# A sequence-mixing, conditioned feed-forward kernel: the fourth half's sum on VectorE, the first remainder on GpSimd, biases ahead of q, two halves scaled in parts

## What is computed

```python
q_emb = relu(cond @ W3 + b3)                       # 128 x 256
v_sum = x.sum(axis=1, keepdims=True)
x1    = (32 * x + v_sum) * q_emb[:, None, :]
c     = relu(x1 @ W2 + b2)
w1q, w3q, w2q = ternary(w1), ternary(w3), ternary(w2)   # clip(round(w / mean|w|), -1, 1) * mean|w|
h1, h3 = c @ w1q.T, c @ w3q.T                      # 682 hidden features
out   = x + (silu(h1) * h3) @ w2q.T
```

## Time and profile before

| | us |
|---|---|
| median of 3 runs | 165.37 (165.34 to 166.15) |
| profiled execution | 165.74 |
| its span, first to last instruction | 163.9 |
| TensorE busy | 159.6 (97% of the span) |
| VectorE busy | 118.7 (72%) |
| ScalarE busy | 89.2 (54%) |
| GpSimd busy | 55.2 (34%) |
| chain of work that ended last | TensorE 97%, VectorE 1% |

### The profile page before, as it was taken

The page is one execution under the profiler, slowest core; times in us unless marked ns, Lnnn a source line. Parts: engine busy times, 40 slices in busy tenths (PEclk is TensorE's granted clock), DMA queues, the critical chain, the costliest instruction groups (busy, mean ns, idle before and its releaser), DMA issues.

```text
span 163.9 us, 2289 instructions
## 1 busy us (share of the span) xinstructions
PE 159.6 (97%) x760; PEld 131.2 (80%) x760; DVE 118.7 (72%) x189; ACT 89.2 (54%) x163; POOL 55.2 (34%) x53
## 2 busy tenths in 40 slices
PE   7899999999999999999999999999999999999992
PEld 3798778888887888788887888788887888788892
DVE  2588999988978891788548891888548870566863
ACT  4068889435844375345844466355844566255540
POOL 5014033402360276205740276204841266001500
PEclk9999999999999999999999999999999999999999
DMA  4998646566566599000250007000150006000163
GB/s 123 342 345 167 97 77 100 94 98 102 84 96 97 91 217 171 2 4 0 38 90 0 0 4 125 5 0 0 30 100 4 2 0 115 13 0 0 19 113 128
DMA packets 67412, 12.67 MB, mean 77 GB/s; under 512 B 63216, under 2 KB 67144, under 8 KB 67400
## 3 DMA queue, kind: packets, MB, share of 16 engines
q1 hardware_dynamic: 67248, 12.46, 38.9%
q10 hardware_dynamic: 152, 0.07, 0.2%
HBM read 8.32 MB, written 4.19 MB: 76 GB/s over the span
## 4 chain that ended last, share of the span: by engine, by line
PE 97%; DVE 1%; issue 0%
PE bank L538 49%; PE bank L581 21%; PE bank L469 17%; PE bank L565 3%; PE bank L503 1%; PE bank L445 1%; PE bank L484 1%; PE bank L452 0%; PE bank L496 0%; DVE x L656 0%; DVE qT L744 0%; PE bank L478 0%; PE bank L443 0%; DVE xo L793 0%; PE bank L506 0%
## 5 line engine op out<-in xcount | busy, mean ns | idle before, releaser
L538 PE MATMUL bank<-c_hi,T 128*128 128x512 f32 (+1 forms) x176 | 69.2, 393 | 0.0
L538 PE MATMUL bank<-c_lo,T 128*128 128x512 f32 (+1 forms) x176 | 68.8, 391 | 0.0
L389 ACT ACTIVATE silu<-bank,checked 128x512 f32<-128x512 f32 (+1 forms) x48 | 33.1, 689 | 51.6 <-PE bank L538 51.4
L778 DVE SCALAR_TENSOR_TENSOR gf<-bank,out_scale,silu 128x512 f32<-128x512 f32 (+1 forms) x42 | 31.2, 744 | 34.5 <-PE bank L538 30.8
L538 PEld LDWEIGHTS bank<-c_hi,T 128*128 128x128 f32 (+1 forms) x176 | 32.8, 186 | 7.6 <-issue 0.2
L538 PEld LDWEIGHTS bank<-c_lo,T 128*128 128x128 f32 (+1 forms) x176 | 32.8, 186 | 7.3
L272 POOL TENSOR_TENSOR x<-y,qT 128x512 f32<-128x512 f32 x12 | 13.7, 1145 | 53.2 <-DVE y L685 53.2
L469 PE MATMUL bank<-x,W_sb 128*128 128x256 f32 x128 | 29.5, 381 | 0.5 <-DVE x L656 0.5
L581 PE MATMUL bank<-g_hi,T 128*128 128x512 f32 x70 | 28.5, 407 | 0.0
L786 DVE TENSOR_TENSOR g_lo<-gf,g_hi 128x512 fp32r<-128x512 f32 x40 | 28.4, 711 | 0.0
L396 ACT CAST g_hi<-gf 128x512 fp32r<-128x512 f32 x40 | 24.5, 612 | 5.4 <-DVE gf L778 5.1
(11 more groups left out here) (78 smaller groups left out, 111.7 us busy)
## 6 DMA issues: line engine op xcount, KB each, us to landing
xb<-in_x_dram SPq DMA_DIRECT2D x64, 64.0 KB, 2.5
out_dram<-turned SPq DMA_DIRECT2D x28, 128.0 KB, 2.7
xo<-in_x_dram SPq DMA_DIRECT2D x3, 256.0 KB, 4.0
w_sb<-in_L_ffn_w_dram SPq DMA_DIRECT2D x2, 384.0 KB, 5.1
w_sb<-in_L_ffn_w_dram SPq DMA_DIRECT2D x1, 682.0 KB, 7.5
w_sb<-in_L_ffn_w_dram SPq DMA_DIRECT2D x2, 256.0 KB
xo<-in_x_dram SPq DMA_DIRECT2D x1, 512.0 KB, 4.2
xo<-in_x_dram SPq DMA_DIRECT2D x2, 128.0 KB, 2.7
```

Source lines behind the costliest of these rows:

```text
L389: nc.scalar.activation(silu[r, m % 2, :], h1[j % 2][r], ACT.Silu, scale=checked[r, 0:1]).then_inc(silu_done, 1)
L538: last = pe.matmul(dst[j % 2][0:w, :], T13[:, k, col:col + w], part[:, g % NC, k, :], start=(i == 0), stop=(i == len(passes) - 1))
L778: nc.vector.scalar_tensor_tensor(out=gf[r, m % 3, :], in0=second, scalar=out_scale[r], in1=silu[r, m % 2, :], op0=ALU.mult, op1=ALU.mult). ...
```

## The change

- `SUMMED` has half 3 too: TensorE only transposes it, VectorE sums it over the sequence, adds the sum and scales it from `y`. This scaling moves ahead of the first limit and comparison.
- The remainder of half 0 moves from VectorE to GpSimd, where it stands behind the two `c_hi` and does not wait for the fourth scaling; the remainder of half 1 still does.
- `transpose_b` stands ahead of `project_q`.
- Halves 0 and 1 are scaled in two instructions of 256 columns, one for each block of features; TensorE starts on the first block (`first_part_done`), and does both blocks' matmuls in that order.
- The fillers read a constant that the launch sets up, and the tile `blank` and its memset go.

```diff
-    SUMMED = (1, 2)
+    SUMMED = (1, 2, 3)
...
                     if n == 0 and t == 1:
+                        transpose_b()
                         project_q()
-                        transpose_b()
...
+            def project_by_parts(n):
+
+                z = z_of(n)
+                for k in range(DC):
+                    if k:
+                        pe.wait_ge(x1_done, n + 1)
+                    else:
+                        pe.wait_ge(first_part_done, n + 1)
+                    for c in range(DC):
+
+                        last = pe.matmul(z[:, c, :], W2_sb[:, k, c * P:(c + 1) * P], x1[:, n % 2, k, :],
+                                         start=(k == 0 and c == 0), stop=(k == DC - 1), skip_group_check=True)
+                last.then_inc(z_done, 1)
...
-            pe.wait_ge(blank_ready, 1)
+            filler = nc.const_aps.tensor(1.0, [P, BANK], BF16)
             for _ in range(WARM_UP):
-                pe.matmul(bank[:, 7, :], blank[:], blank[:].unsqueeze(1).broadcast_to([P, BANK // P, P]), start=True, stop=True)
+                pe.matmul(bank[:, 7, :], filler[:, 0:P], filler, start=True, stop=True)
...
-            project_c(0)
+            project_by_parts(0)
             mix_x(2)
-            project_c(1)
+            project_by_parts(1)
...
+            def scale_by_parts(n):
+
+                if n in SUMMED:
+                    dve.wait_ge(y_done, nth_summed(n))
+                else:
+                    dve.wait_ge(mixed_done, n + 1)
+                for k, done in enumerate((first_part_done, x1_done)):
+                    whole = y[:, n % 2, k] if n in SUMMED else mixed_of(n)[:, k * HT:(k + 1) * HT]
+                    nc.vector.tensor_tensor(by_batch(x1[:, n % 2, k]), by_batch(whole),
+                                            qT[:, n, k].unsqueeze(2).broadcast_to([P, HB, S]), ALU.mult).then_inc(done, 1)
```

More of the change, by code:

```diff
@@ L99, in adaln_ternary_ffn_kernel @@
         mix = sb("mix", [P, P], F32)
-        blank = sb("blank", [P, P], BF16)
         warm = sb("warm", [P, 1], F32)
@@ L160, in adaln_ternary_ffn_kernel @@
         zeroed = sem("zeroed")
-        blank_ready, mix_ready = sem("blank_ready"), sem("mix_ready")
+        mix_ready = sem("mix_ready")
+        first_part_done = sem("first_part_done")
         condT_done, condT_copied = sem("condT_done"), sem("condT_copied")
@@ L282, in _ @@
                 nc.gpsimd.tensor_copy(half_of(c_hi, n), ct[:, n % NCT]).then_inc(first_hi_done, 1)
-            pool.wait_ge(early_lo_done, 1)
-            pool.wait_ge(x1_done, EARLY)
-            for n in range(1, EARLY):
+            for n in range(EARLY):
+                if n == 1:
+                    pool.wait_ge(x1_done, EARLY)
                 if n < HALVES:
@@ L508, in keep_busy @@
                 for _ in range(n):
-                    pe.matmul(bank[:, 7, 0:P], blank[:], blank[:], start=True, stop=True)
+                    pe.matmul(bank[:, 7, 0:P], filler[:, 0:P], filler[:, 0:P], start=True, stop=True)
             keep_busy(2)
@@ L681, in add_sum @@
                 dve.wait_ge(vsum_done, nth_summed(n))
-                if n >= EARLY:
-                    dve.wait_ge(x1_done, max(n - 1, SUMMED[-1] + 1))
+                if n > HALVES:
+                    dve.wait_ge(x1_done, n - 1)
                 nc.vector.scalar_tensor_tensor(
@@ L728, in check_scales @@
                                                ).then_inc(checked_done, 1)
-            nc.vector.memset(blank[:], 0.0).then_inc(blank_ready, 1)
             nc.vector.memset(mix[:], 0.0).then_inc(mix_ready, 1)
@@ L747, in _ @@
             parts = [slice(part[0] * D, (part[-1] + 1) * D) for part in PARTS]
-            scale_mixed(0)
+            scale_by_parts(0)
             for n in SUMMED:
@@ L751, in _ @@
                 add_sum(n)
-                scale_mixed(n)
-            early_lo(0)
+                if n < HALVES:
+                    scale_by_parts(n)
+                else:
+                    scale_mixed(n)
             limit(0)
             above_limit(0, w1_sb, w1_t, parts[0])
-            scale_mixed(3)
             limit(1)
```

4 lines of the change are left out of this document (removed).

## The result

| | before | changed |
|---|---|---|
| median of 6 runs, us | 165.91 (165.34 to 166.16) | 168.88 (168.02 to 169.62) |
| ratio, 95% interval | 1 | 1.0188 [1.0164, 1.0212] |
| profiled execution, us | 165.74 | 169.16 |
| its span, us | 163.9 | 167.4 |
| TensorE busy, us | 159.6 | 160.6 |

The changed kernel is 3.0 us slower. I had forecast 166.5 with a range up to 168.3. Its chain of work that ended last is TensorE 95% and VectorE 3%, where it was 97% and 1%.

What follows compares the result with a forecast made beforehand. TensorE, busy from the first hidden product at 16.71, bounds the end, so only earlier work matters. One hold puts that product 1.20 or 1.04 later, about 1.15 on 165.37: 166.5 us, range 165.6 to 168.3.

Steps and rivals of the forecast that it cites:

- project(0): TensorE's projection of half 0, after the first scaling at the launch; forecast to start at 6.87, 0.51 us sooner.
- two holds: Rival: GpSimd's remainders block both scale(3) and the first comparison on VectorE; 2.29 us later, 167.7 us, chance 0.35.
- the hand-over: TensorE's transpose of w1_t's first part, which waits for the first comparison; 14.19 before, forecast 15.57.
- the first hold: On VectorE, scale(3) waits until GpSimd is through with half 0's remainder; costs 1.02 us read as a lock.
- the longer chain: VectorE's added sum, addition and scaling of half 3 ahead of the first comparison; priced at 0.86 us to the hand-over.
- The new wait: Behind the hand-over: second comparison perhaps held until 16.7, ending 17.25, needed at 17.7; nothing new was forecast late.
- the second race: Whether GpSimd's second remainder (14.79) or VectorE's first comparison (14.83) starts first; GpSimd's lead 0.04 us.
- one hold: Main case: GpSimd's remainder blocks VectorE's path once, about 1.15 us; 166.5 us, chance 0.45.
- scale(3): VectorE's scaling of half 3, now from y in SBUF, ahead of the comparison; forecast about 1.7 us instead of 0.69.
- the fall of the clock: Rival: TensorE's standstill of 2 to 3 us drops its clock, up to 2 us more; 169.6 with two holds, chance 0.05.
- the launch: Work up to project(0): q's reordering makes the first scaling start 0.26 sooner, part scaling brings the gain to 0.51 us.
- Rivals 2 and 3: 2: GpSimd doesn't stop the comparison, 165.5 us, chance 0.12. 3: TensorE's earlier arrival counts in full, 164.5, faster 0.03.

Runs made afterwards that it cites:

- the longer chain alone: Kernel before with half 3 summed on VectorE and scaled ahead of the comparison, half 0's remainder on VectorE behind it: ratio 1.0076, median 166.86 us.
- the launch parts alone: Kernel before with only fillers on constants, biases ahead of q and halves 0 and 1 scaled in parts: ratios 0.9985 and 1.0008, medians 165.67 and 165.70 us.
- The repeated profile: The changed kernel run again unedited for a second profile: profiled execution 168.52 us, ratio 1.0172 over its first three executions.

## Why the prediction was wrong

**What held.** The end moves with the first hidden product: from there to the end of the span it was 147.2 and 147.7, the half microsecond being the rest of the clock's spell. VectorE's comparison became what TensorE waits for. From project(0) the way was well forecast: for two holds I had worked out 16.66 - 6.87 = 9.79 from project(0) to the hand-over; it was 9.77 and 9.78 in the two profiles. That it fits to 0.02 is in part luck, since two errors cancel: the first hold was priced at 1.02 and the second at 1.09 (16.60 - 15.51), and they measured 0.95 and 0.97; the longer chain was priced at 0.86 (14.54 - 6.87 = 7.67, where before it was 6.81) and measured 1.00 and 1.04. From hand-over to hidden product I had 2.34; it was 2.42 where the clock stayed up. The new wait that I looked for behind the hand-over didn't appear with two holds, and did when they were gone.

**The step that failed: the second race.** I took one hold as the likeliest (0.45) and two as a rival (0.35), because the second remainder would start 0.15 behind scale(3)'s end and only 0.04 ahead of the comparison. The 0.15 came from the earlier trace rows (14.48 to 14.63). In the changed kernel the remainder starts 0.08 after scale(3) is through (12.46 + 1.69 = 14.15, 14.23), and so 0.09 ahead of the comparison, as far as in the race that GpSimd wins in the earlier trace rows (12.72 and 12.82). All five profiles with both holds say the same: a lead of 0.13 for the first, of 0.08 or 0.09 for the second. Why the gap is 0.08 and not 0.15 stays open. The remainder waits for two semaphores where it waited for three, but their number is not enough: with the longer chain alone it waits for three, and starts 0.09 behind the end of what releases it (14.98 + 0.69 = 15.67, 15.76). In the four profiles with 0.14 or 0.15 the releasing scale(3) reads PSUM, in those with 0.07 to 0.09 the releasing instruction reads SBUF only; no run changes that alone. With two holds as the forecast the time would have been 167.7, still within the range; what took the time out of it are the next two.

**The second: the fall of the clock.** It had 0.05 and was left outside the range. Its price was about right (up to 2.0; in the first profile 1.06 up to the hidden product, 3.48 less 2.42, and 0.5 behind it; but the three executions at 0.980 took 3 us more than those beside them). Its chance was far too small: by the mean clock six of twelve executions have it. And it should have been tied to the holds, since it was seen only with their standstill. The range's end at 168.3 leaves out four of the six executions without a fall, and all with one.

**The third: the launch.** Project(0) was forecast at 6.87, 0.51 sooner. The profiles with all launch parts give 6.41, 7.30, 6.41, 6.68, 6.95, 6.88 and 7.79, with the launch parts alone 7.36 and 7.50; the kernel before gives 7.38 and its variants 7.40, 6.83 and 7.26. I read one execution as if the pace's rise and the transfers stood still. The way from q's product to project(0) did become 0.54 shorter, as worked out; but what lies ahead of it and the transfers moved by more, and alone the launch parts gave ratios of 0.9985 and 1.0008. The repeated profile shows what this does to the sum: project(0) at 7.30 in place of 6.87 and the hidden product at 19.50 in place of 19.00. The forecast for two holds would have been 168.2 with that, and 168.5 without the 0.37 that I took off because the first three times of the kernel before had a median of 165.37; over six it is 165.91, and the profiled execution with 165.74 is an ordinary one. That is the 168.51 of the middle of the executions without a fall. That the fillers on constants don't bring the rise forward was the value taken; with fillers alone the ratio was 1.0012, and nothing measured speaks against it.

**Rivals 2 and 3** (no hold; earlier arrival counts in full) are out: both holds are there, and even without them the chain costs 1.00.

## What to carry to other kernels

An operation moved to another engine is free only against what that engine's neighbour does at that moment: here a remainder on GpSimd cost nothing beside a scaling that reads PSUM, and 0.95 us beside the same scaling reading SBUF. When two waits end within a tenth of a microsecond of each other, a gap read at another place (0.15 there, 0.08 here) can't tell which ends first, so price both outcomes and let the range hold the worse one with its delays. And where a forecast lets TensorE stand still, as here for 1.9 and 2.9 us, give that a second price: 8 of 19 executions had a lower mean clock, and in the one of them that was profiled the work behind the standstill ran at half the clock for some 3.4 us.

## What the runs showed of the hardware that I had not expected

- A lead of 0.09 us is enough: GpSimd's remainder, started that much before VectorE's comparison, held it for its whole length (1.72 us instead of 0.75). With VectorE 0.19 ahead, GpSimd was the one that waited (two remainders in 2.94 us, the comparison 0.77).
- A held instruction of VectorE ends 0.54 or 0.55 behind GpSimd's recorded end, whatever it takes alone: scale(3) at 14.15 behind 13.60 (0.69 alone), the comparison at 16.04 behind 15.49 (0.75 alone). So a part of it, 0.14 or 0.20, isn't held, or GpSimd's recorded end is late by that; the traces don't tell which.
- In the profiled execution of the changed kernel TensorE had been without work for most of 13.4 to 16.2 and the granted clock was 0.51 from 17.5 to 21.0, over a microsecond after work had begun again. In another execution with the same standstill it stayed at 1.00. Mean clocks come in steps: near 1.00, 0.990 and 0.980, the last only in the last three of six executions on one chip.
- q's four matmuls at the launch took from 0.61 to 1.22 us, by execution and not by kernel (0.71 and 1.16 in the two profiles of the changed kernel), with the recorded clock at 1.00 in every case.
- W2 came late enough to hold up project(0) by 0.89 and 0.96 us in two of the profiles.
